# The causal mask of an attention block: from a product on TensorE to an addition in VectorE's copy of the diagonal strip

## The chip, the cores and the metric

The kernel runs on one core of a Trainium2 chip, as one program in one launch. The metric is the device time in microseconds. Five engines with queues of their own work side by side and wait for each other on semaphores: TensorE (products, PE), VectorE (DVE), ScalarE (ACT), GpSimd (POOL) and SyncE (SP), which issues the transfers.

## The reference

One transformer block with adaptive layer normalisation, on 2048 tokens of 512 features. The attention part, cut to what matters:

```python
q = einsum('bpm,hmd->bphd', x, Q_w) + Q_b        # 16 heads of 128
k = einsum('bpm,hmd->bphd', x, K_w) + K_b
v = einsum('bpm,hmd->bphd', x, V_w) + V_b
logits = einsum('bqhd,bkhd->bhqk', q, k) / sqrt(128)
logits = where(triu(ones((s, s)), k=1), -100000.0, logits)   # no query sees a later key
scores = softmax(logits, axis=-1)
attn = einsum('bhqk,bkhd->bqhd', scores, v)
out = einsum('bqhd,hdm->bqm', attn, O_w) + O_b
```

A second normalisation and a feed-forward part follow: a router that picks 4 of 64 experts per token, the experts, and two shared experts.

## The kernel before

Products of 32-bit accuracy are made of three: each operand is split into a high and a low part, and `matmul3` (L1551 to L1553) adds high by high, high by low and low by high. The probabilities and values are split in the same way into two 16-bit parts.

The attention runs head by head, and in a head in four stages, j = 0 to 3, one for each block of 512 queries. A stage has four rows, t = 0 to 3, of 128 queries. A row's logits come in j + 1 strips, one for each block of 512 keys; each strip is one PSUM bank, and four banks (`strip`) are used in turn. The last strip of a row, ch = j, lies on the diagonal: it has only (t + 1) x 128 columns, and of these the last 128 need the mask. Strips are counted over a head, 40 in all: 4, 8, 12 and 16 in the stages.

TensorE in stage (h, j) does `score(h, j)`, then `sum_values` for the stage before it (probabilities by values, into `pv`), then the projections q, k and v of the stage after it. `score` waits for `strip_out` before each strip, that is, until VectorE has copied the strip that was in that bank four strips ago, and raises `strip_done` after it. In a diagonal strip a fourth product, `ident_bf` by `mask_bf`, adds the mask's -1e5/scale above the diagonal of the last 128 columns (L1606).

VectorE in `score_row` copies each strip to `exps` (SBUF) and scales it, and takes its maximum by the way into `cmax`; the maximum is read out by a second instruction, DVE_READ_ACCUMULATOR. It then joins the maxima of the row. ScalarE takes the exponentials and their sum (L860) and makes the high part of the probabilities (`p_hi`, L869); VectorE makes the low part (`p_lo`, L1163). After the rows VectorE splits the low parts of the next q and k and of the next values (L1122, L1126, L1129).

SP issues the transposing transfers of the probabilities into `pT` (L476), 4 (j + 1) of them in a stage, strictly in order: those of rows 0 and 1, then those of rows 2 and 3. `pT` has four slots, and before the high part of rows 0 and 1 goes into a slot, SP waits on `pv_group` until the values have been summed over what the slot held. A `wait_alone` is an instruction of its own that waits and then counts a semaphore up. `sum_values` waits on `p_turned` for the slot it reads.

At the start GpSimd makes the constants `ident`, `ident_bf` and `mask_bf`. Much later, in the feed-forward part, `h2_tmp` holds a block for the second normalisation's split, `wr_sb` the router's weights, and SP loads the weights of the shared experts chunk by chunk (`load_chunk`).

Of the kernel before, what the change touches and what calls it, by code (L numbers as in the profile page):

```python
# [16 lines left out]
F32 = mybir.dt.float32  # L17
F32R = mybir.dt.float32r
BF16 = mybir.dt.bfloat16
# [3 lines left out]
ALU = mybir.AluOpType  # L23
ACT = mybir.ActivationFunctionType
AX_X = mybir.AxisListType.X
P = 128
# [15 lines left out]
def adaln_block(nc, x, Q_w, Q_b, K_w, K_b, V_w, V_b, O_w, O_b, Wr, router_bias, Wg, Wu, Wd, Sg, Su, Sd,  # L42
# [3 lines left out]
    E, _, HE = Wg.shape  # L46
# [3 lines left out]
    NT = S // P  # L50
    DC = D // P
    QB = S // 512
    TB = 4
    SC = NS * HS // P
    EPS = 1e-5
    SCALE = float(DH) ** -0.5
    MASKED = -1e5 / SCALE
# [7 lines left out]
    with ExitStack() as ctx:  # L65
        def sem(name):
            return ctx.enter_context(nc.semaphore(name))
# [4 lines left out]
        STRIPS, GENS, PTS = 4, 3, 4  # L72
        PSCALE, VMOST = 2.0 ** 14, 2.0 ** 14
        strip = [bank(f"strip{i}") for i in range(STRIPS)]
# [4 lines left out]
        base = (nc.sbuf_base + 63) // 64 * 64  # L79
        keep = SbufMap(nc, base)  # L80
        ident = keep.place("ident", [P, P], F32)
        ident_bf = keep.place("ident_bf", [P, P], BF16)
        mask_bf = keep.place("mask_bf", [P, P], BF16)
        modT = keep.place("modT", [P, 6 * DC], F32)
        scale_a = keep.place("scale_a", [P, DC], F32)
        scale_b = keep.place("scale_b", [P, DC], F32)
# [9 lines left out]
        cmax = keep.place("cmax", [P, TB, QB], F32)  # L96
# [36 lines left out]
        exps = a.place("exps", [P, TB, S], F32)  # L133
# [5 lines left out]
        spare_at = a.at  # L139
# [31 lines left out]
        o = SbufMap(nc, kqv_at)  # L171
# [5 lines left out]
        assert o.at <= v16_at, o.at  # L177
        acc = SbufMap(nc, pT_at).place("acc", [P, NT, D], F32)
        assert spare_at - pT_at >= NT * D * 4
        o = SbufMap(nc, spare_at)  # L180
        h2_tmp = o.place("h2_tmp", [P, 512], F32)
        assert o.at <= nc.sbuf_usable_end, o.at


        h2T_hi = SbufMap(nc, halves_at).place("h2T_hi", [P, DC, S], F32R)
# [6 lines left out]
        f = SbufMap(nc, w_at)  # L192
        n2 = f.place("n2", [P, 1, TB, D], F32)
        o_tmp = f.place("o_tmp", [P, D], F32)
        wr_sb = f.place("wr_sb", [P, DC, E], F32)
        s_raw = [SbufMap(nc, kqv_at - 3 * D * 4).place("s_raw0", [P, 3, D], F32)]
        assert f.at <= kqv_at - 3 * D * 4

# [2 lines left out]
        f = SbufMap(nc, kqv_at)  # L201
# [5 lines left out]
        f = SbufMap(nc, v16_at)  # L207
        s_hi[0] = f.place("s_hi0", [P, 3, D], F32R)
        s_lo[0] = f.place("s_lo0", [P, 3, D], F32R)
        assert f.at <= exps_at  # L210

        f = SbufMap(nc, hT_at)
# [62 lines left out]
        consts = sem("consts")  # L275
# [2 lines left out]
        mod_mm, mod_out = sem("mod_mm"), sem("mod_out")  # L278
        dve_step = sem("dve_step")
        pool_step = sem("pool_step")  # L280
        pool_waited, sp_waited = sem("pool_waited"), sem("sp_waited")
        tile_stat = sem("tile_stat")
        ln_stats, ln_rstd, ln_norm = sem("ln_stats"), sem("ln_rstd"), sem("ln_norm")
        ln_turned, ln_mod, ln_split = sem("ln_turned"), sem("ln_mod"), sem("ln_split")
# [5 lines left out]
        strip_done, strip_out = sem("strip_done"), sem("strip_out")  # L290
# [15 lines left out]
        wr_hi_ready, wr_split = sem("wr_hi_ready"), sem("wr_split")  # L306
# [68 lines left out]
        NSTRIP = strips_before(QB)  # L375
# [59 lines left out]
        def _(sp):  # L435
# [150 lines left out]
            h, j = H - 1, QB - 1  # L586
# [37 lines left out]
            store_n2(3)  # L624
            sp.wait_ge(ln_turned, 2 * NT)
            sp.wait_ge(n2_stored, 16 * QB)
            sp.wait_ge(wr_split, 1)
            load_chunk(3)
            load_chunk(4)

# [42 lines left out]
        def _(pool):  # L673
            steps = [0]

            def link(ins):
                steps[0] += 1
                ins.then_inc(pool_step, 1)
                pool.wait_ge(pool_step, steps[0])

            def wait_alone(semaphore, value):
# [5 lines left out]
            link(nc.gpsimd.memset(ident[:], 0.0))  # L687
            nc.gpsimd.affine_select(out=ident[:], in_=ident[:], compare_op=ALU.not_equal, fill=1.0, base=0,
                                    pattern=[[-1, P]], channel_multiplier=1).then_inc(consts, 1)
            link(nc.gpsimd.memset(ident_bf[:], 0.0))  # L690
            nc.gpsimd.affine_select(out=ident_bf[:], in_=ident_bf[:], compare_op=ALU.not_equal, fill=1.0, base=0,
                                    pattern=[[-1, P]], channel_multiplier=1).then_inc(consts, 1)
            link(nc.gpsimd.memset(mask_bf[:], 0.0))
            nc.gpsimd.affine_select(out=mask_bf[:], in_=mask_bf[:], compare_op=ALU.is_ge, fill=MASKED, base=0,
                                    pattern=[[-1, P]], channel_multiplier=1).then_inc(consts, 1)
            nc.gpsimd.memset(neghalf[:], -0.5).then_inc(consts, 1)

# [30 lines left out]
                nc.gpsimd.tensor_copy(bias_now[:], src).then_inc(bias_ready, 1)  # L728

            pool.sem_inc(v_bound, 1)  # L730
            pool.wait_ge(consts, 4)
            ln_scales(0, 0)
            pool.wait_ge(mod_out, 1)
            nc.gpsimd.tensor_copy(bias_now[:], biasT[:].rearrange("p (n h) -> p n h", n=3)[:, :, 0]
# [330 lines left out]
        def _(dve):  # L1065
# [67 lines left out]
            def value_scale(h, src):  # L1133
# [4 lines left out]
                dve.wait_ge(v_scaled_half, h + 1)  # L1138
                nc.vector.reciprocal(v_scale[:], v_most[:]).then_inc(v_scaled, 1)

            def score_row(h, j, t):
                for ch in range(j + 1):
                    u = strips_before(j) + t * (j + 1) + ch
                    w = 512 if ch < j else (t + 1) * P
                    dve.wait_ge(strip_done, h * NSTRIP + (u + 1))
                    nc.vector.tensor_scalar(exps[:, t, 512 * ch:512 * ch + w], strip[u % STRIPS][:, 0:w], SCALE, None,  # L1146
                                            ALU.mult, ALU.max, accum_out=cmax[:, t, ch:ch + 1]).then_inc(strip_out, 1)
                dve.wait_ge(strip_out, h * NSTRIP + (STRIPS + u + 1))
                nc.vector.tensor_reduce(nbias[:, t:t + 1], cmax[:, t, 0:j + 1], AX_X, ALU.max, negate=True  # L1149
                                        ).then_inc(row_logits, 1)  # L1150
# [147 lines left out]
            h, j = H - 1, QB - 1  # L1298
# [115 lines left out]
            def route_experts(s):  # L1414

                m = tiles_of(s)
                if s == 0:
                    dve.wait_ge(consts, 7)
                    link(nc.vector.tensor_copy(iota_f[:], iota_i[:]))
                for t in range(half * s, half * s + half):  # L1420
                    steps[0] += 1
                    nc.vector.max_index(idx[:, t, :], vals[:, t, :], scores[:, t, :]).then_inc(dve_step, 1)
                dve.wait_ge(dve_step, steps[0])
                link(nc.vector.tensor_copy(idx_f[:, m], idx[:, m, 0:TOPK]))
                for k in range(TOPK):
                    link(nc.vector.tensor_tensor(onehot[k][:, m], iota_f[:, 0:E].unsqueeze(1).to_broadcast([P, half, E]),
                                                 idx_f[:, m, k:k + 1].to_broadcast([P, half, E]), ALU.is_equal))
                dve.sem_inc(experts_known, 1)
# [119 lines left out]
        def _(pe):  # L1548
# [46 lines left out]
            def score(h, j):  # L1595
                pe.wait_ge(gen_out, nth("k", j, h) + GENS)
                for n, (t, ch, w) in enumerate(score_units(j)):
                    u = strips_before(j) + n
                    pe.wait_ge(strip_out, h * NSTRIP + (u + 1))
                    o = strip[u % STRIPS]  # L1600
                    rows, cols = slice(P * t, P * t + P), slice(512 * ch, 512 * ch + w)
                    last = matmul3(o[:, 0:w], qT_hi[:, rows], qT_lo[:, rows], kT_hi[:, cols], kT_lo[:, cols],
                                   True, True)
                    if ch == j:

                        last = nc.tensor.matmul(o[:, w - P:w], ident_bf[:], mask_bf[:], start=False, stop=True,  # L1606
                                                skip_group_check=True)
                    last.then_inc(strip_done, 1)

            def sum_values(h, j):  # L1610
# [37 lines left out]
                    project("v", jn, hn)  # L1648


            pe.wait_ge(consts, 4)
            pe.wait_ge(rows_landed, 48)
            nc.tensor.transpose(pv[:, 0:3 * H], bias_rows[:], ident[0:3 * H, 0:3 * H]).then_inc(mod_mm, 1)
            pe.wait_ge(c_step, 1)
# [253 lines left out]
```

## Time and profile before

| | us |
|---|---|
| median of 3 runs | 2125.84 |
| lowest and highest run | 2123.46 and 2131.11 |
| the profiled execution's own time | 2127.13 |
| its span, first to last instruction | 2125.3 |

The profile is of one execution. PE is the product engine, PEld its weight loads, which overlap products; the stated busy time of products overlaps too, since each is counted until its result is out. Busy times therefore tell which engine is full, and the distances between starts tell what an instruction costs. A row of a timeline gives start and duration in us, engine, line, operation, output and inputs, and in square brackets the idle time before it with what ended it. SPq is SP's queue, where an issue of a transfer takes time.

### The profile page before, as it was taken

How to read it: one execution, taken by the hardware profiler on the slowest of the kernel's cores; microseconds unless marked ns; L12 is line 12 of the kernel's file. 1: busy time of each engine (PE TensorE's matmuls, PEld its weight loads, DVE VectorE, ACT ScalarE, POOL GpSimd, SP SyncE). 2: the span in 40 equal slices, each digit the busy share in tenths (PEclk: the TensorE clock that was granted, in tenths of full speed). 3: DMA queues.
4: the chain of work that ended last, by engine and by line, in shares of the span. 5: the costliest groups of instructions: out<-in, count | busy, mean ns of one | idle time of the engine just before them, and what ended most of it. 6: DMA issues, size and time to landing. Idle time of an engine off the chain costs nothing.

```text
span 2125.3 us, 33337 instructions
## 1 busy us (share of the span) xinstructions
PE 2028.7 (95%) x10121; PEld 1513.4 (71%) x10121; DVE 1382.4 (65%) x3219; ACT 1106.3 (52%) x1638; POOL 387.0 (18%) x411
## 2 busy tenths in 40 slices
PE   6899999999999999999999999999999989999996
PEld 3667677676677676676776766767887768777775
DVE  7677686686686776866866866846555933333375
ACT  4566675675575665756765756533334134344310
POOL 5211010110110110100101101524001132222364
PEclk9999999999999999999999999999999999999998
DMA  6487788888878878887888889995422089999664
GB/s 213 94 163 154 158 159 162 161 157 162 168 153 168 167 153 166 160 162 159 159 162 158 161 162 176 185 205 178 135 83 65 1 253 289 318 291 319 195 206 149
DMA packets 932174, 366.08 MB, mean 172 GB/s; under 512 B 754800, under 2 KB 885920, under 8 KB 932128
## 3 DMA queue, kind: packets, MB, share of 16 engines
q1 hardware_dynamic: 921888, 331.93, 69.3%
q0 software_dynamic: 10240, 33.56, 5.1%
q8 instruction: 26, 0.43, 0.1%
q14 instruction: 20, 0.16, 0.0%
HBM read 138.86 MB, written 41.94 MB: 85 GB/s over the span
## 4 chain that ended last, share of the span: by engine, by line
PE 66%; SPq 14%; DMA 8%; DVE 5%; POOL 3%; issue 3%; ACT 1%; POOLq 0%; DVEq 0%; ACTq 0%
SPq L476 13%; PE gen L1551 9%; PE gen L1553 9%; PE gen L1552 9%; PE strip L1551 7%; PE strip L1553 7%; PE strip L1552 7%; PE pv L1551 4%; PE strip L1847 4%; PE pv L1553 4%; PE pv L1552 4%; DMA wd_sb<-in_L_ffn_Wd 3%; DMA pT<-p_lo 2%; PE strip L1854 2%; DVE acc L1533 1%
## 5 line engine op out<-in xcount | busy, mean ns | idle before, releaser
L1163 DVE SCALAR_TENSOR_TENSOR p_lo<-exps,rinv,p_hi 128x512 f16<-128x512 f32 (+3 forms) x256 | 395.6, 1560 | 23.2 <-ACT p_hi L869 21.2
L860 ACT ACTIVATE exps<-exps,nbias 128x128 f32<-128x128 f32 (+15 forms) x256 | 306.2, 1197 | 131.9 <-DVE nbias L1149 130.5
L1146 DVE TENSOR_SCALAR_CACHE_REDUCE exps<-strip 128x512 f32<-128x512 f32 (+3 forms) x640 | 359.4, 606 | 1.9 <-PE strip L1606 1.3
L869 ACT ACTIVATE p_hi<-exps,rinv 128x512 f16<-128x512 f32 (+3 forms) x256 | 338.0, 1351 | 9.5 <-DMA pT<-p_lo 3.7
L1551 PE MATMUL strip<-kT_hi,qT_hi 128*128 128x512 f32 (+3 forms) x640 | 247.7, 387 | 10.3 <-DVEq L1240 6.3
L1551 PE MATMUL pv<-pT,v 128*128 128x512 f16 (+3 forms) x640 | 222.9, 348 | 19.3 <-DMA pT<-p_lo 19.1
L1553 PE MATMUL strip<-kT_hi,qT_lo 128*128 128x512 f32 (+3 forms) x640 | 233.9, 366 | 0.0
L1552 PE MATMUL strip<-kT_lo,qT_hi 128*128 128x512 f32 (+3 forms) x640 | 233.4, 365 | 0.0
L715 POOL TENSOR_TENSOR wq_lo<-wq_raw,wq_hi 128x512 fp32r<-128x512 f32 x16 | 20.8, 1297 | 1117.8 <-ACT wq_hi L839 1117.8
L1552 PE MATMUL pv<-pT,v 128*128 128x512 f16 (+3 forms) x640 | 222.6, 348 | 0.0
L1553 PE MATMUL pv<-pT,v 128*128 128x512 f16 (+3 forms) x640 | 219.5, 348 | 0.0
L1551 PEld LDWEIGHTS strip<-kT_hi,qT_hi 128*128 128x128 f32 x640 | 122.8, 192 | 36.4 <-DVE exps L1146 7.7
L1036 ACT ACTIVATE xbT<-gen,modT,scale_b 128x128 f32<-128x128 f32 x256 | 96.3, 457 | 92.7 <-PE gen L1839 92.7
L1553 PEld LDWEIGHTS strip<-kT_hi,qT_lo 128*128 128x128 f32 x640 | 120.8, 189 | 18.8
L1122 DVE SCALAR_TENSOR_TENSOR qT_lo<-gen,bias_now,qT_hi 128x512 fp32r<-128x512 f32 x64 | 47.8, 747 | 132.6 <-ACT qT_hi L846 132.6
L1552 PEld LDWEIGHTS strip<-kT_lo,qT_hi 128*128 128x128 f32 x640 | 121.6, 190 | 17.1
L1129 DVE SCALAR_TENSOR_TENSOR vT<-gen,v_scale,vT 128x512 f16<-128x512 f32 x64 | 48.0, 750 | 125.8 <-ACT vT L854 125.6
L1551 PEld LDWEIGHTS pv<-pT,v 128*128 128x128 f16 x640 | 62.7, 98 | 89.8 <-DMA pT<-p_lo 37.1
L1491 DVE TENSOR_TENSOR hE<-strip,sil_e 128x128 f32<-128x128 f32 x64 | 18.7, 292 | 154.1 <-ACT sil_e L1043 154.1
L854 ACT ACTIVATE vT<-gen,v_scale 128x512 f16<-128x512 f32 x64 | 44.1, 688 | 136.5 <-PE gen L1553 132.8
L1551 PE MATMUL gen<-hT_hi,a_hi 128*128 128x512 f32 x256 | 101.7, 397 | 9.6 <-DVE a_lo L1282 6.1
L1551 PE MATMUL gen<-hT_hi,wq_hi 128*128 128x512 f32 x256 | 106.5, 416 | 1.8 <-issue 1.8
(240 smaller groups left out, 4410.4 us busy)
## 6 DMA issues: line engine op xcount, KB each, us to landing
at_dram<-at_f SPq DMA_DIRECT2D x64, 256.0 KB, 2.6
wg_sb<-in_L_ffn_Wg SPq DMA_DIRECT2D x64, 256.0 KB, 5.1
wu_sb<-in_L_ffn_Wu SPq DMA_DIRECT2D x64, 256.0 KB, 5.4
wd_sb<-in_L_ffn_Wd SPq DMA_DIRECT2D x64, 256.0 KB, 6.1
yb_dram<-yb SPq DMA_DIRECT2D x64, 256.0 KB, 6.0
a_f<-at_dram SPq DMA_DIRECT2D x58, 256.0 KB, 2.8
pT<-p_hi SPq DMA_TRANSPOSE x320, 3.3
pT<-p_lo SPq DMA_TRANSPOSE x320, 3.3
```

The costliest lines, as they stand in the source:

```text
L476: sp.dma_start_transpose(out, rows).then_inc(p_turned[slot_of(j, g)], 16)
L860: nc.scalar.activation(row, row, ACT.Exp, bias=nbias[:, t:t + 1], accum_out=rsum[:, t:t + 1]).then_inc(row_probs, 1)
L869: nc.scalar.activation(p_hi16[:, 0:j + 1, t, :], row, ACT.Copy, scale=rinv[:, t:t + 1]).then_inc(p_hi, 1)
L1036: ins = nc.scalar.activation(xbT[:, i % 2, P * ch:P * ch + P], e_turn[:, P * ch:P * ch + P], ACT.Identity, bias=modT[:, 3 * DC + ch:3 * DC ...
L1122: ins = nc.vector.scalar_tensor_tensor(qT_lo[:], src[:], bias_now[:, 0:1], qT_hi[:].bitcast(F32), ALU.add, ALU.subtract)
L1129: ins = nc.vector.scalar_tensor_tensor(vT16[:, 1, :], src[:], v_scale[:, 0:1], vT16[:, 0, :], ALU.mult, ALU.subtract)
L1146: nc.vector.tensor_scalar(exps[:, t, 512 * ch:512 * ch + w], strip[u % STRIPS][:, 0:w], SCALE, None, ALU.mult, ALU.max, accum_out=cmax[:, ...
L1163: nc.vector.scalar_tensor_tensor(p_lo16[:, 0:j + 1, t, :], row, rinv[:, t:t + 1], p_hi16[:, 0:j + 1, t, :], ALU.mult, ALU.subtract).then_i ...
L1551: nc.tensor.matmul(o, a_hi, b_hi, start=start, stop=False)
L1552: nc.tensor.matmul(o, a_hi, b_lo, start=False, stop=False)
L1553: return nc.tensor.matmul(o, a_lo, b_hi, start=False, stop=stop)
L1847: last = nc.tensor.matmul(e_gateup[i % 2][:, P * n:P * n + P], w[:, i % EX, c, :], xbT[:, i % 2, P * c:P * c + P], start=c == 0, stop=c == ...
```

## The change

The mask leaves TensorE. `causal` is a constant of 4 x 128 columns in bfloat16: zeros, and in its last 128 columns the mask. For a diagonal strip of w columns VectorE now uses an operation with two inputs: the strip plus the last w columns of `causal`, times the scale, with the running maximum as before. The wait for the strip is an instruction of its own ahead of it. The other strips are copied as before. `ident_bf` and `mask_bf` are gone; `causal` takes 512 bytes more per partition than both, and so `h2_tmp` and `wr_sb` move into other buffers. Since `h2_tmp` now lies where chunk 3 of the shared weights lands, SP waits for the last split of the second normalisation before it loads that chunk.

```diff
-        ident_bf = keep.place("ident_bf", [P, P], BF16)
-        mask_bf = keep.place("mask_bf", [P, P], BF16)
+        causal = keep.place("causal", [P, TB * P], BF16)
...
-        o = SbufMap(nc, spare_at)
-        h2_tmp = o.place("h2_tmp", [P, 512], F32)
...
-        wr_sb = f.place("wr_sb", [P, DC, E], F32)
+        h2_tmp = f.place("h2_tmp", [P, 512], F32)
...
+        wr_sb = f.place("wr_sb", [P, DC, E], F32)
...
-            sp.wait_ge(wr_split, 1)
+            sp.wait_ge(ln_split, 2 * NT)
             load_chunk(3)
...
-            link(nc.gpsimd.memset(ident_bf[:], 0.0))
-            nc.gpsimd.affine_select(out=ident_bf[:], in_=ident_bf[:], compare_op=ALU.not_equal, fill=1.0, base=0,
-                                    pattern=[[-1, P]], channel_multiplier=1).then_inc(consts, 1)
-            link(nc.gpsimd.memset(mask_bf[:], 0.0))
-            nc.gpsimd.affine_select(out=mask_bf[:], in_=mask_bf[:], compare_op=ALU.is_ge, fill=MASKED, base=0,
+            diagonal = causal[:, (TB - 1) * P:TB * P]
+            link(nc.gpsimd.memset(causal[:], 0.0))
+            nc.gpsimd.affine_select(out=diagonal, in_=diagonal, compare_op=ALU.is_ge, fill=MASKED, base=0,
                                     pattern=[[-1, P]], channel_multiplier=1).then_inc(consts, 1)
...
+            def wait_alone(semaphore, value):
+
+                dve.wait_ge(semaphore, value)
+                dve.sem_inc(dve_waited, 1)
+
             def score_row(h, j, t):
                 for ch in range(j + 1):
                     u = strips_before(j) + t * (j + 1) + ch
                     w = 512 if ch < j else (t + 1) * P
-                    dve.wait_ge(strip_done, h * NSTRIP + (u + 1))
-                    nc.vector.tensor_scalar(exps[:, t, 512 * ch:512 * ch + w], strip[u % STRIPS][:, 0:w], SCALE, None,
-                                            ALU.mult, ALU.max, accum_out=cmax[:, t, ch:ch + 1]).then_inc(strip_out, 1)
+                    if ch < j:
+                        ...
+                    else:
+
+                        wait_alone(strip_done, h * NSTRIP + (u + 1))
+                        nc.vector.tensor_tensor_reduce(exps[:, t, 512 * ch:512 * ch + w], strip[u % STRIPS][:, 0:w],
+                                                       causal[:, TB * P - w:TB * P], SCALE, -3e38, ALU.add, ALU.max,
+                                                       cmax[:, t, ch:ch + 1]).then_inc(strip_out, 1)
...
-                    if ch == j:
-
-                        last = nc.tensor.matmul(o[:, w - P:w], ident_bf[:], mask_bf[:], start=False, stop=True,
-                                                skip_group_check=True)
                     last.then_inc(strip_done, 1)
```

## Rows read from the trace of the kernel before

**Rows 1.** The page: busy time of TensorE, and the chain that ended last, by engine.
```profile
PE 2028.7 (95%) x10121; PEld 1513.4 (71%) x10121; DVE 1382.4 (65%) x3219; ACT 1106.3 (52%) x1638; POOL 387.0 (18%) x411
...
PE 66%; SPq 14%; DMA 8%; DVE 5%; POOL 3%; issue 3%; ACT 1%; POOLq 0%; DVEq 0%; ACTq 0%
```

**Rows 2.** Stretches: stretch, length, busy time by engine, PEclk; a middle and the last head.
```profile
479.24:562.17 82.93, 81.65 (x405) 59.04 (x404) 60.76 (x158) 53.00 (x69) 7.00 (x6) 1.00 0.82 161
1316.90:1399.80 82.90, 75.10 (x363) 55.16 (x361) 62.55 (x135) 47.55 (x57) 43.20 (x32) 1.00 0.96 202
```

**Rows 3.** The chain in order of time, stage 3 and after: start, us, what.
```profile
553.81 0.07 PE pv L1553
...
553.97 1.23 SPq L476
...
570.45 3.16 DMA pT<-p_lo
...
573.66 0.39 PE pv L1551
```

**Rows 4.** Timeline of TensorE in stage 3 around a mask between two rows.
```profile
541.23 0.23 PE L1606 MATMUL strip<-mask_bf,ident_bf 128*128 128x128 bf16 x1
541.26 0.48 PE L1551 MATMUL strip<-kT_hi,qT_hi 128*128 128x512 f32 x1
...
542.05 0.39 PE L1551 MATMUL strip<-kT_hi,qT_hi 128*128 128x512 f32 x1
...
542.74 0.39 PE L1551 MATMUL strip<-kT_hi,qT_hi 128*128 128x512 f32 x1
```

**Rows 5.** The same timeline at the end of stage 3's strips.
```profile
546.83 0.23 PE L1606 MATMUL strip<-mask_bf,ident_bf 128*128 128x128 bf16 x1
546.89 0.38 PE L1551 MATMUL pv<-pT,v 128*128 128x512 f16 x1
```

**Rows 6.** Timelines of TensorE and VectorE at the fifth strip of stages 1 and 2.
```profile
502.85 0.23 PE L1606 MATMUL strip<-mask_bf,ident_bf 128*128 128x128 bf16 x1
503.12 0.50 PE L1551 MATMUL strip<-kT_hi,qT_hi 128*128 128x512 f32 x1
...
502.98 0.08 DVE L1146 DVE_READ_ACCUMULATOR exps<-strip 128x1 f32 x1
...
518.38 0.44 PE L1551 MATMUL strip<-kT_hi,qT_hi 128*128 128x512 f32 x1
...
518.19 0.08 DVE L1146 DVE_READ_ACCUMULATOR exps<-strip 128x1 f32 x1
```

**Rows 7.** Timelines of SP and VectorE in stage 3.
```profile
548.62 6.58 SPq L476 DMA_TRANSPOSE pT<-p_hi  x4
...
554.18 4.61 DVE L1163 SCALAR_TENSOR_TENSOR p_lo<-exps,rinv,p_hi 128x2048 f16<-128x2048 f32 x2 [0.65 <-ACT p_hi L869]
```

**Rows 8.** The chain in order of time: a lone wait in SP's queue.
```profile
560.82 0.02 SPq L439
560.84 0.05 issue
```

**Rows 9.** Groups by line and shape: busy us, mean ns of one, idle before.
```profile
L1146 DVE TENSOR_SCALAR_CACHE_REDUCE exps<-strip 128x512 f32<-128x512 f32 x448 | 289.6, 685 | 0.6 <-PE strip L1553 0.6
...
L1497 DVE TENSOR_TENSOR yb<-strip,gb_bc 128x512 f32<-128x512 f32 x64 | 44.2, 690 | 14.5 <-PE strip L1854 14.3
...
L1352 DVE TENSOR_TENSOR hs_lo<-sil_s,hs_hi 128x512 fp32r<-128x512 f32 x32 | 22.6, 706 | 12.6 <-ACT hs_hi L995 12.6
...
L1146 DVE TENSOR_SCALAR_CACHE_REDUCE exps<-strip 128x128 f32<-128x128 f32 x64 | 18.2, 285 | 0.6 <-PE strip L1606 0.6
```

**Rows 10.** Timelines of VectorE and TensorE, first strip of row 3 in stage 3.
```profile
543.55 0.08 DVE L1146 DVE_READ_ACCUMULATOR exps<-strip 128x1 f32 x1
...
544.00 0.47 PE L1551 MATMUL strip<-kT_hi,qT_hi 128*128 128x512 f32 x1
```

**Rows 11.** Timelines of SP and VectorE at the shared weights' chunk 3.
```profile
1604.33 0.37 SPq L582 DMA_DIRECT2D s_raw<-in_L_ffn_Sg  x1
...
1608.16 0.69 DVE L1252 TENSOR_TENSOR h2T_lo<-h_tmp,h2T_hi 128x512 fp32r<-128x512 f32 x1 [1.58 <-ACT h_tmp L976]
```

More of the change, by code:

```diff
@@ L179, in adaln_block @@
         assert spare_at - pT_at >= NT * D * 4
-        o = SbufMap(nc, spare_at)
-        h2_tmp = o.place("h2_tmp", [P, 512], F32)
-        assert o.at <= nc.sbuf_usable_end, o.at
         h2T_hi = SbufMap(nc, halves_at).place("h2T_hi", [P, DC, S], F32R)
@@ L280, in adaln_block @@
         pool_step = sem("pool_step")
-        pool_waited, sp_waited = sem("pool_waited"), sem("sp_waited")
+        pool_waited, sp_waited, dve_waited = sem("pool_waited"), sem("sp_waited"), sem("dve_waited")
         tile_stat = sem("tile_stat")
@@ L730, in _ @@
             pool.sem_inc(v_bound, 1)
-            pool.wait_ge(consts, 4)
+            pool.wait_ge(consts, 3)
             ln_scales(0, 0)
@@ L1144, in score_row @@
                     w = 512 if ch < j else (t + 1) * P
-                    dve.wait_ge(strip_done, h * NSTRIP + (u + 1))
-                    nc.vector.tensor_scalar(exps[:, t, 512 * ch:512 * ch + w], strip[u % STRIPS][:, 0:w], SCALE, None,
-                                            ALU.mult, ALU.max, accum_out=cmax[:, t, ch:ch + 1]).then_inc(strip_out, 1)
+                    if ch < j:
+                        dve.wait_ge(strip_done, h * NSTRIP + (u + 1))
+                        nc.vector.tensor_scalar(exps[:, t, 512 * ch:512 * ch + w], strip[u % STRIPS][:, 0:w], SCALE,
+                                                None, ALU.mult, ALU.max, accum_out=cmax[:, t, ch:ch + 1]
+                                                ).then_inc(strip_out, 1)
+                    else:
[3 more added lines that the diff above has]
+                                                       cmax[:, t, ch:ch + 1]).then_inc(strip_out, 1)
                 dve.wait_ge(strip_out, h * NSTRIP + (STRIPS + u + 1))
@@ L1417, in route_experts @@
                 if s == 0:
-                    dve.wait_ge(consts, 7)
+                    dve.wait_ge(consts, 6)
                     link(nc.vector.tensor_copy(iota_f[:], iota_i[:]))
@@ L1648, in stage @@
                     project("v", jn, hn)
-            pe.wait_ge(consts, 4)
+            pe.wait_ge(consts, 3)
             pe.wait_ge(rows_landed, 48)
```

## The prediction

> **What bounds the kernel now.** I read the page first: TensorE is busy 95% of the span, and the chain of work that ended last runs 66% through TensorE and 14% through SP's own queue [rows 1]. TensorE is therefore the first suspect, but the second share says that somewhere it waits for transfers. The stretches say where the change acts: the masks exist only in the attention of 16 heads, and a head from the middle, 479.24 to 562.17, takes 82.93 us with TensorE at its full granted clock (1.00), busy 81.65 us, VectorE only 60.76 [rows 2]. Then I followed the chain through that head. It leaves TensorE at one place: when the value products of stage 2's probabilities end (553.81 + 0.07), SP may reuse the slot of transposed probabilities and issues stage 3's fourth transpose at 553.97; 12 more follow back to back, the last at 570.45, landing 3.16 us later, and only then, at 573.66, does TensorE go on [rows 3]. In between TensorE did other work (the next head's projections and its four score strips of stage 0) and then stood, so that work is not on the chain. A head is a ring: TensorE from 573.66 through stages 1, 2 and 3 up to the end of the stage-2 values, then SP. A saving counts if it falls in the TensorE part of the ring.
>
> **What the change removes on TensorE.** 16 mask products per head, 4 in each stage. Their busy time is no price, since products overlap. The starts give it. A mask starts at 541.23, the next row's first product at 541.26, which is 0.03; that next strip then takes 542.05 - 541.26 = 0.79, where a strip after no mask takes 542.74 - 542.05 = 0.69 [rows 4]. The 0.10 is the weight load of the next row, which the short mask product is too short to cover. So a mask between two rows costs 0.03 + 0.10 = 0.13 us. The last mask of a stage is followed by a value product 0.06 later [rows 5] and I find no second term there: 0.06.
>
> The Trainium skill bears on the first figure: "TensorE: Matmul & The Clock Gate", section "Back-to-back issue gap", gives about 81 ns per product of 128 columns in a stream of load and product pairs, where the trace shows 0.13. By that page the eight masks counted below would be worth 8 x 0.08 x 15 = 9.7 us; I keep the trace.
>
> **Which masks are on the ring.** Stage 0's four lie in the stretch that ends in the wait for the transposes: nothing. In stages 1 to 3 VectorE starts to copy strips only after it has split the projected values that come in just before them, and there are four strip banks, so the fifth strip waits for the first to be copied. In stage 1 a mask starts at 502.85 and the next strip only at 503.12, 0.06 after the accumulator read that frees its bank ends (502.98 + 0.08) [rows 6]. Masks ahead of that point only make TensorE arrive earlier at the same gate: rows 0 and 1 in stage 1, row 0 in stage 3 likewise. In stage 2 the fifth strip starts at 518.38, 0.11 after its bank came free (518.19 + 0.08) [rows 6]: 0.05 could be won there, but TensorE would then have the next weights loaded only when the gate opens, as in stage 1, so I put nothing. What is left: stage 1, one mask between rows and the last, 0.13 + 0.06 = 0.19; stage 2, two between and the last, 0.32; stage 3 likewise 0.32. Together 0.83 us per head. Both ends of this term: 8 x 0.03 = 0.24 if only the masks' own slots count, and 12 x 0.13 + 4 x 0.06 = 1.8 if all 16 do.
>
> Does the saving in stage 3 pass on to SP? SP's first four transposes there take 6.58 us from 548.62 [rows 7]; four of 1.23 (the fourth's length [rows 3]) are 4.92, and the rest, 1.66 with three gaps, is mostly waiting for value groups. There is more than 0.32 to take back. The rows that follow are not late either: the last two parts of the probabilities are ready at 554.18 + 4.61 = 558.79, while the transposes that need them come after 560.8 [rows 7, 8].
>
> **What it adds on VectorE.** 16 copies per head change from a one-input operation with a running maximum (685 ns for 512 columns, 285 for 128) to a two-input one with scaling and a maximum. The trace of before has no such operation. The nearest rows are two-input ones from the same kind of bank: 690 ns for 512 columns [rows 9]. I take 5 ns more. Bounds: below, the 0.08 of the accumulator read could go; above, half rate: the slope is (685 - 285) / 384 = 1.04 ns per column, so up to 0.53 more at 512 columns and 0.13, 0.27, 0.40 at the narrower ones. The lone wait ahead of each copy is one more instruction. SP's, of the same make, take 0.02 with 0.05 behind them [rows 8]; VectorE's queue is ahead of its datapath while it copies back to back, so I take 0, bounds 0 and 0.07. What hides VectorE's extra: it is 60.76 busy in 82.93, and before each stage's strips it stands for the value part; and no gate strip above is a diagonal one. Where cover ends is the tightest bank behind the gate: in stage 3 the strip at 544.00 uses a bank freed at 543.55 + 0.08, a slack of 0.37 [rows 10]. With the masks gone TensorE comes 0.16 sooner (one whole mask, 0.13, and one slot, 0.03), and 0.06 is the least gap, so VectorE may be 0.15 late there. Two diagonal copies lie before it, so each may cost 0.07 more for nothing: with my 0.005 the loss is zero, and so it is with the whole 0.07 of the lone wait.
>
> **The rest of the diff.** GpSimd makes two constants instead of three before VectorE's first statistics: both hide behind the load of the input, 0. SP's chunk 3 of the shared weights now waits for the last split of the second normalisation: the load went at 1604.33, the split ends at 1608.16 + 0.69, so 4.5 us later [rows 11]. Queued behind it on SP are chunk 4, which waits for a later split anyway, and the expert loads, which wait for routing; the chunk is first read in step 10 of the twelve that begin there. 0, and if it delayed chunk 4 it would be a microsecond. The moved buffers carry the same transfers.
>
> **Sum.** The ring exists for heads 0 to 14: 15 x 0.83 = 12.5 us. Head 15 has its weights for the output projection loading between the transposes and GpSimd busy 43.20 us instead of 7.00; TensorE is busy only 75.10 of 82.90 there [rows 2], so I put 0. The profiled execution took 2127.13 (span 2125.3), which gives 2114.6; the median of the three times is 2125.84, 1.3 below the profiled one, which gives 2113.3. I say 2113.
>
> **Rivals.**
> All masks count: if the wait at 573.66 shrinks too and the gates move, 16 heads at 1.8 give 29 us, 2097. Against: the gates' 0.06 and the twelve back-to-back transposes, which no mask touches.
> Stage 3 gives nothing, because SP or ScalarE is late by then and the ring's SP part starts no sooner: 0.51 x 15 = 7.7, 2118. For it: everything SP does in stage 3 is queued in order. Against: the time SP spends waiting in its first four [rows 7].
> The new operation runs at half rate. Then 0.13 + 0.27 = 0.40 come before the tight strip against 0.15 allowed, a loss of 0.25 in stage 3, taken to be the same in stage 2, none in stage 1: 0.83 - 0.50 = 0.33 a head, 5.0 us, 2121. Against: a subtraction with both inputs in SBUF takes 706 ns for 512 columns [rows 9], no half rate. The Trainium skill warns of this: "Vector Engine (DVE) Microarchitecture Reference", section "Points that are easy to get wrong", says that one kind of instruction with two non-bf16 SBUF sources halves its throughput. Here one source is a PSUM bank and the other is bf16, so by its own words it need not bind, and the trace does not show it.
> Slower: a fixed cost x per diagonal copy, from a slow start of this new kind of operation or from a wait that VectorE's queue cannot run ahead of. It holds back the strips at the tight banks: 2x - 0.15 in stages 2 and 3, and x - 0.15 in stage 1 (one diagonal copy before the strip behind the gate, slack taken alike), together 5x - 0.45 against 0.83: it decides from x = 0.26 us. At x = 0.5 the head loses 1.2 us, 18 in all, 2144. Against: all of VectorE's known operations on such a bank have the same fixed part: 0.285 less 128 x 1.04 ns is 0.15, and 0.690 less 512 x 1.04 ns is 0.16 [rows 9].
> That the masks are really gone from TensorE is plain from the diff.
>
> **Chances.** Forecast 0.54, all masks 0.07, stage 3 gives nothing 0.14, half rate 0.13, slower 0.09, and 0.03 for what I don't see. A measurement of this kernel tells 0.5%, 10.6 us, from no change, so faster means below 2115.2. Of the forecast's own range, 2109 to 2117, about four fifths lie there. Faster 0.43 + 0.07 = 0.50; same: a fifth of the forecast, 0.11, with stage 3 and half rate, 0.27, and part of the unseen, 0.40; slower 0.10. The range 2102 to 2126 leaves out the slower case and the far end of the full saving.
>
> **What would show it.** The strip behind a row's end should take 0.69 instead of 0.79 and start where the mask did; the fifth strip of stages 1 to 3 should still start 0.06 after its bank is freed; a head should take 82.1 us; TensorE's stand before the last value group of stage 3 should grow, since stage 0's masks now go into it. The diagonal copy should read about 690 ns at 512 columns. If a head is at 82.93 with VectorE's strips late, the operation is dear; if it is near 81, the gates are not what I take them for.

## The result, and the profile after

Over four executions each, shared on one chip, the changed kernel takes 2113.12 us (median; 2111.54 to 2119.06), the kernel before 2125.95 (2123.46 to 2131.11). The ratio is 0.9942, 95% interval 0.9914 to 0.9969: faster by 0.6%. The forecast was 2113, from 2102 to 2126. The profiled execution of after happens to be its slowest, 2119.06, so the time is compared by heads below and not by the two spans.

The page, busy time of TensorE and VectorE and the chain by engine (answers to [rows 1]):
```profile
PE 2014.0 (95%) x9863; PEld 1501.2 (71%) x9865; DVE 1381.3 (65%) x3219; ACT 1103.8 (52%) x1638; POOL 386.7 (18%) x409
...
PE 65%; SPq 15%; DMA 8%; DVE 4%; issue 4%; POOL 3%; ACT 1%; DVEq 0%; POOLq 0%; ACTq 0%
```
258 TensorE records fewer (256 of them would be the masks), and the chain has the same shape: TensorE gave up 14.7 us of busy time, VectorE's is the same to 1.1 us.

The two stretches of [rows 2]: the middle head, from its first score strip to the next head's, and the last head, where the stretch is taken as long and as far behind the head's first strip (8.4 us) as in before.
```profile
473.11:555.39 82.28, 80.66 (x389) 58.17 (x388) 60.70 (x158) 52.89 (x69) 7.00 (x6) 1.00 0.83 163
1304.13:1387.03 82.90, 75.30 (x350) 55.56 (x348) 62.36 (x135) 47.43 (x57) 42.05 (x32) 0.98 0.94 200
```
The middle head went from 82.93 to 82.28 (82.1 was forecast). The last head's first strip starts at 1295.77 instead of 1308.54, so 12.8 us are won by then. Behind it the profiled execution gives 4.7 back: 821.5 us to its end against 816.8. That part takes 816 to 822 in the profiles of this study, whatever the kernel, so one execution does not say whose it is.

The ring of [rows 3], in the chain of waits of the same head:
```profile
547.04 0.07 PE pv L1561
...
547.20 1.23 SPq L473
...
563.72 3.31 DMA pT<-p_lo
...
567.08 0.39 PE pv L1559
```
It is unbroken: stage 2's values end, SP issues 13 transposes, TensorE goes on 0.04 behind the last landing. From the fourth transpose to there it is 19.88 us, before 19.69: SP's part did not get shorter.

TensorE's timeline in stage 3 around the place where the mask between two rows was (answers to [rows 4]), and at the end of its strips [rows 5]:
```profile
534.64 0.28 PE L1561 MATMUL strip<-kT_hi,qT_lo 128*128 128x256 f32 x1
534.76 0.40 PE L1559 MATMUL strip<-kT_hi,qT_hi 128*128 128x512 f32 x1
...
535.46 0.40 PE L1559 MATMUL strip<-kT_hi,qT_hi 128*128 128x512 f32 x1
...
536.14 0.39 PE L1559 MATMUL strip<-kT_hi,qT_hi 128*128 128x512 f32 x1
...
539.88 0.39 PE L1561 MATMUL strip<-kT_hi,qT_lo 128*128 128x512 f32 x1
540.12 0.39 PE L1559 MATMUL pv<-pT,v 128*128 128x512 f16 x1
```
The strip that opens a row takes 535.46 - 534.76 = 0.70 where it took 0.79: the exposed weight load is gone with the mask. The weight loads themselves say it too, before and after:
```profile
541.23 0.20 PEld L1551 LDWEIGHTS strip<-kT_hi,qT_hi 128*128 128x128 f32 x1
```
```profile
534.64 0.19 PEld L1559 LDWEIGHTS strip<-kT_hi,qT_hi 128*128 128x128 f32 x1
```
The load for the row's first product starts 0.03 before that product in before (541.26) and 0.12 before it in after (534.76).

The gates at the fifth strip of stages 1 and 2, TensorE and VectorE (answers to [rows 6]):
```profile
497.15 0.50 PE L1559 MATMUL strip<-kT_hi,qT_hi 128*128 128x512 f32 x1 [0.19 <-DVE exps L1147]
...
512.18 0.51 PE L1559 MATMUL strip<-kT_hi,qT_hi 128*128 128x512 f32 x1
```
```profile
497.01 0.08 DVE L1147 DVE_READ_ACCUMULATOR exps<-strip 128x1 f32 x1
...
512.04 0.08 DVE L1147 DVE_READ_ACCUMULATOR exps<-strip 128x1 f32 x1
```
Stage 1's strip starts 0.06 after the read that frees its bank, as before; stage 2's now does too (0.06, before 0.11). The masks ahead of a gate bought nothing.

VectorE's copies by form (busy us, mean ns of one; answers to [rows 9]), and the first strip of row 3 in stage 3 with the read that frees its bank [rows 10]:
```profile
L1147 DVE TENSOR_SCALAR_CACHE_REDUCE exps<-strip 128x512 f32<-128x512 f32 x384 | 249.1, 685 | 1.8 <-PE strip L1561 1.8
...
L1153 DVE CUSTOM_DVE_ANT_0 exps<-strip,causal 128x512 f32<-128x512 f32 x64 | 44.0, 687 | 1.5 <-PE strip L1561 0.3
...
L1153 DVE CUSTOM_DVE_ANT_0 exps<-strip,causal 128x384 f32<-128x384 f32 x64 | 35.4, 553 | 1.4
...
L1153 DVE CUSTOM_DVE_ANT_0 exps<-strip,causal 128x256 f32<-128x256 f32 x64 | 26.9, 421 | 1.7 <-PE strip L1561 0.2
...
L1153 DVE DVE_READ_ACCUMULATOR2_ANT cmax<- 128x1 f32 x256 | 21.2, 83 | 0.0
...
L1153 DVE CUSTOM_DVE_ANT_0 exps<-strip,causal 128x128 f32<-128x128 f32 x64 | 18.2, 284 | 0.6 <-PE strip L1561 0.6
```
```profile
537.08 0.08 DVE L1147 DVE_READ_ACCUMULATOR exps<-strip 128x1 f32 x1
...
537.35 0.40 PE L1559 MATMUL strip<-kT_hi,qT_hi 128*128 128x512 f32 x1
```
The new operation takes 687 ns for 512 columns beside 685 for the plain copy, and 284 for 128 where it was 285. The slack at the tight bank is 537.35 - 537.16 = 0.19, where it was 0.37: half used up, not gone.

To see where the time came from, each stage is measured from its first score strip to the next stage's, mean over heads 2 to 14, worked out from the starts in the trace of each run. The last column is the chip's ratio to the kernel before.

```
kernel                        stage 0   1      2      3     head   time     ratio [95%]
before                        21.47  15.22  20.36  25.88   82.93  2125.95
after                         21.59  15.02  20.04  25.58   82.24  2113.12  0.9942 [0.9914, 0.9969]
e1_again                      21.55  15.02  20.05  25.56   82.19  2115.12  0.9934 [0.9921, 0.9948]
e2_no_mask                    21.55  15.02  20.05  25.57   82.19  2113.73  0.9925 [0.9912, 0.9939]
e3_hidden8                    21.56  15.02  20.06  25.57   82.21  2115.58  0.9936 [0.9922, 0.9949]
e4_ring8                      21.55  15.21  20.35  25.89   83.00  2128.79  0.9998 [0.9988, 1.0008]
e5_both                       21.58  15.20  20.36  25.89   83.04  2127.87  1.0004 [0.9994, 1.0015]
e6_delay64                    21.57  15.01  20.32  26.22   83.12  2129.32  1.0008 [0.9996, 1.0021]
e7_delay320                   21.56  15.85  20.33  26.75   84.49  2153.18  1.0128 [1.0106, 1.0150]
e8_late_after                 20.14  15.02  20.05  25.58   80.79  2094.46  0.9852 [0.9836, 0.9869]
e9_q_first                    19.61  16.73  20.05  25.58   81.96  2116.41  0.9947 [0.9934, 0.9960]
e10_q_first_old_mask          20.05  17.64  20.35  25.90   83.93  2146.02  1.0082 [1.0067, 1.0097]
e11_q_first_stage0            20.05  17.10  20.05  25.58   82.77  2124.77  0.9983 [0.9971, 0.9995]
e12_values_later              19.61  15.52  20.04  26.74   81.90  2108.70  0.9903 [0.9889, 0.9917]
```
In e10 and e11 the means mix two kinds of heads, as shown with them. e1 to e4 shared a chip and runs of before with median 2129.4, e5 to e8 2128.12, e9 to e12 2128.61; times of different groups are compared by ratio.

### The profile page after: what moved, and what is told of

It reads as the page before. It is cut to its first block, busy times and chain, and to the rows that moved or that the text cites. A ratio compares the mean times of both kernels' runs of the same rounds, so it can differ in the third digit from the quotient of the medians.

```text
span 2117.3 us, 33076 instructions
## 1 busy us (share of the span) xinstructions
PE 2014.0 (95%) x9863; PEld 1501.2 (71%) x9865; DVE 1381.3 (65%) x3219; ACT 1103.8 (52%) x1638; POOL 386.7 (18%) x409
## 4 chain that ended last, share of the span: by engine, by line
PE 65%; SPq 15%; DMA 8%; DVE 4%; issue 4%; POOL 3%; ACT 1%; DVEq 0%; POOLq 0%; ACTq 0%
SPq L473 14%; PE gen L1559 9%; PE gen L1561 9%; PE gen L1560 9%; PE strip L1559 7%; PE strip L1560 6%; PE strip L1561 6%; PE strip L1851 4%; PE pv L1559 4%; PE pv L1561 3%; PE pv L1560 3%; DMA wd_sb<-in_L_ffn_Wd 3%; DMA pT<-p_lo 2%; PE strip L1858 2%; DVE acc L1541 1%
## 5 line engine op out<-in xcount | busy, mean ns | idle before, releaser
L1559 PE MATMUL strip<-kT_hi,qT_hi 128*128 128x512 f32 (+3 forms) x640 | 238.3, 372 | 14.4 <-DVEq L1248 6.3
L1147 DVE TENSOR_SCALAR_CACHE_REDUCE exps<-strip 128x512 f32<-128x512 f32 x384 | 249.1, 685 | 1.8 <-PE strip L1561 1.8
L1153 DVE CUSTOM_DVE_ANT_0 exps<-strip,causal 128x128 f32<-128x128 f32 (+3 forms) x256 | 124.5, 486 | 5.2 <-PE strip L1561 1.1
```

Of the source, the lines that this page charges most:

```text
L1153: nc.vector.tensor_tensor_reduce(exps[:, t, 512 * ch:512 * ch + w], strip[u % STRIPS][:, 0:w], causal[:, TB * P - w:TB * P], SCALE, -3e38, ...
L1559: nc.tensor.matmul(o, a_hi, b_hi, start=start, stop=False)
```

## The experiments

**The changed kernel once more** (e1), for a firmer interval beside the others. 

> The changed kernel once more, for a firm ratio. Ring theory (only masks behind the fifth strip of stages 1, 2 and 3 count): a head takes 82.2 us, 0.7 less than before, and the time is 12 us below the kernel before, about 2114. Rival (the first measurement was luck of the feed-forward part, where two executions differ by some us): the ratio comes out at 0.998 or above.


Measured: 2115.12, ratio 0.9934. The first result stands, a head is 82.19.

**No mask on either engine** (e2): the kernel before, with the product left out. Its output lacks the causal mask.
```diff
-                    if ch == j:
-                        last = nc.tensor.matmul(o[:, w - P:w], ident_bf[:], mask_bf[:], start=False, stop=True,
-                                                skip_group_check=True)
```


> The kernel before without the mask product, and no mask anywhere: VectorE copies as before. This is the gain of TensorE's part alone. If VectorE's new operation costs nothing: the same as the changed kernel, 2114, a head 82.2. If the new operation and its lone wait give part of the gain back: below the changed kernel, by 0.07 x 5 x 15 = 5 us or more.


Measured: 82.19 a head, ratio 0.9925 [0.9912, 0.9939], e1's 0.9934 [0.9921, 0.9948]. The intervals overlap: VectorE's mask with its lone waits, the fewer constants and the moved buffers cost nothing that can be measured. The traces of before and after say the same: VectorE's copies of stage 3 take 9.674 and 9.671 us from the start of the first to that of the last.

**Eight masks back on TensorE ahead of the gates** (e3), **or eight behind them** (e4), on top of VectorE's own. The product adds the zero part of the constant, so it has the old size and changes no value.
```diff
                                    True, True)
+                    if ch == j and t <= (3, 1, 0, 0)[j]:    # e4: t > (3, 1, 0, 0)[j]; e5: always
+                        last = nc.tensor.matmul(o[:, w - P:w], causal[:, 0:P], causal[:, 3 * P:4 * P], start=False,
+                                                stop=True, skip_group_check=True)
                     last.then_inc(strip_done, 1)
```


> The changed kernel with a product of the mask's size that adds zeros put back in 8 of 16 rows: all of stage 0, rows 0 and 1 of stage 1, row 0 of stages 2 and 3. Ring theory: these are ahead of a gate or of the wait for the transposes, so nothing, a head 82.2, 2114. Rival (every mask product costs the same share of TensorE's time): half of the gain goes, a head 82.6, 2120.

> The changed kernel with the same product put back in the other 8 rows: rows 2 and 3 of stage 1, rows 1 to 3 of stages 2 and 3. Ring theory: the whole gain goes, a head 82.9, 2126. Rival (equal shares): half, a head 82.6, 2120.


A head of each, from its first strip to the next head's:
```profile
473.85:556.19 82.34, 80.84 (x397) 58.68 (x396) 60.70 (x158) 52.89 (x69) 7.00 (x6) 1.00 0.83 162
```
```profile
476.73:559.76 83.03, 81.45 (x397) 58.51 (x396) 60.77 (x158) 53.00 (x69) 7.00 (x6) 1.00 0.82 161
```
Both run 397 products; they differ only in where the eight stand. The first eight cost 0.02 a head by the table (82.21 beside 82.19), the other eight 0.81 (83.00), and 0.19, 0.30 and 0.33 of it lie in stages 1, 2 and 3. On the chip e3 keeps the whole gain and e4 has none of it. This is what set the ring apart from a plain sum over products, by which both would have lost the same. The Trainium skill's "TensorE: Matmul & The Clock Gate", section "Back-to-back issue gap", would make the eight 8 x 0.081 = 0.65; the heads of e3 and e4 differ by 0.79 in the table, so here the page's figure comes out too small. By [rows 4] and [rows 5] one figure does not fit both places: the five between rows are priced at 0.13, the three at a stage's end at 0.06, together 0.83.

**All sixteen back** (e5), the new VectorE operation kept. 

> The changed kernel with a product that adds zeros put back in all 16 rows, so that only VectorE's side differs from the kernel before. If VectorE's side costs nothing: as before, 2126, a head 82.9. If the new operation costs x more than the 0.1 or so that the tightest banks have to give: above, by 5x a head.


Measured: 83.04 a head, ratio 1.0004. The whole gain is the products'; nothing else in the diff has a part of it that the interval, 0.9994 to 1.0015, would show.

**A dearer diagonal copy** (e6 and e7): a small VectorE addition between the lone wait and the copy, 64 or 320 columns, into a buffer that nothing reads.
```diff
                         wait_alone(strip_done, h * NSTRIP + (u + 1))
+                        nc.vector.tensor_tensor(junk[:, 0:64], ga_bc[:, 0:64], gb_bc[:, 0:64], ALU.add)   # e7: 0:320
                         nc.vector.tensor_tensor_reduce(...
```


> The changed kernel with an addition of 64 columns on VectorE, into a scratch buffer, ahead of each of the 16 diagonal copies of a head: x = 64 x 1.04 ns + 0.07 = 0.14 us each. Ring theory with the slacks read in the changed kernel (first strip of row 3: 0.19 in stage 3, second strip of row 3: 0.16 in stage 2, least gap 0.06, two diagonal copies ahead of each): 2x - 0.13 + 2x - 0.10 = 0.33 a head, 5 us, 2118. If VectorE, busy three quarters of a head, has room: 0. If its work were all on the path: 16x = 2.2 a head, 33 us.

> The same with 320 columns: x = 0.40 us. Ring theory: 2x - 0.13 and 2x - 0.10 in stages 3 and 2, x - 0.27 in stage 1, 1.5 a head, 23 us, 2137, slower than the kernel before; the break-even lies near x = 0.23. With room on VectorE: 0. All on the path: 6.4 a head, 96 us.


Measured: ratios 1.0008 and 1.0128; against the changed kernel a head loses 0.9 and 2.3 us. The slower rival's mechanism is real. The strips that it names now start the instant their bank is free: the slack at row 3's first strip in stage 3, 0.19 in the changed kernel, is 0.055 in both. The loss sits in stages 2 and 3 for e6 (0.28 and 0.64, expected 0.18 and 0.15). For e7 it is 0.83, 0.29 and 1.17 in stages 1, 2 and 3, where 0.13, 0.70 and 0.67 were expected: both sums came out too small, and e7's was also placed wrongly. The groups of the added operation, busy us and mean ns of one:
```profile
L1154 DVE TENSOR_TENSOR junk<-ga_bc,gb_bc 128x64 f32<-128x64 f32 x256 | 66.8, 261 | 2.9 <-PE strip L1563 0.6
```
```profile
L1154 DVE TENSOR_TENSOR junk<-ga_bc,gb_bc 128x320 f32<-128x320 f32 x256 | 131.2, 512 | 2.8 <-PE strip L1563 0.6
```
From its start to the next operation's it takes 0.138 and 0.404 us as a median (worked out from the starts), the sizes meant. But e6 loses more than such a size gives, and for stage 3 the reason is in two of the sixteen additions, rows 0 and 2. VectorE and GpSimd at row 2:
```profile
544.27 0.60 DVE L1154 TENSOR_TENSOR junk<-ga_bc,gb_bc 128x64 f32<-128x64 f32 x1
544.79 0.55 DVE L1155 CUSTOM_DVE_ANT_0 exps<-strip,causal 128x384 f32<-128x384 f32 x1
```
```profile
543.48 1.30 POOL L711 TENSOR_TENSOR wv_lo<-wv_raw,wv_hi 128x512 fp32r<-128x512 f32 x1
```
The addition took 0.60 instead of 0.22, and the copy behind it starts at 544.79, as GpSimd's subtraction ends (543.48 + 1.30 = 544.78). The addition reads two tensors of SBUF while GpSimd reads two. The Trainium skill states this ("SBUF — State Buffer", section "Terms": the pair of ports that the two engines share is held for the full instruction, and the loser "fully blocks"), and by these rows the trace agrees. It does not at row 1, where the GpSimd operation reads one tensor of SBUF only:
```profile
540.35 1.92 POOL L718 TENSOR_SCALAR wv_abs<-wv_raw 128x512 bf16<-128x512 f32 x1
...
541.42 0.22 DVE L1154 TENSOR_TENSOR junk<-ga_bc,gb_bc 128x64 f32<-128x64 f32 x1
```
The addition lies wholly inside that operation and takes its usual 0.22, in each of the 15 heads where the two meet. So the measurement decides for a narrower rule: held up beside a two-input operation of GpSimd, not beside this one-input one. The new copy reads one bank and one SBUF tensor and was never held up: the longest of 256 took 693 ns, and 34 of them overlap a two-input subtraction of GpSimd. So in stage 3 row 0's addition cost 0.38 and row 2's 0.52 in place of 0.14, by VectorE's row lengths (2.654 against 2.277, 3.360 against 2.844). Why stage 2 lost 0.10 more than expected stays open.

e7's loss in stage 1 comes mostly by a wait that the expectation had not counted. TensorE at the first strip of stage 2:
```profile
522.30 0.39 PE L1563 MATMUL gen<-hT_hi,wv_lo 128*128 128x512 f32 x1
523.05 0.49 PE L1561 MATMUL strip<-kT_hi,qT_hi 128*128 128x512 f32 x1 [0.36 <-DVE kT_lo L1122]
```
VectorE, late by then, has not split the low part of k, and TensorE takes 0.75 from start to start where such products follow each other in 0.23: 0.52 of the 0.83, and the like in each of heads 2 to 14 (0.33 to 0.38 idle there, none in after).

**Where stage 0's masks went** (e8). In the trace of after TensorE stands before the last value group of stage 3, and that is where the time freed in stage 0 ends:
```profile
565.45 0.38 PE L1561 MATMUL pv<-pT,v 128*128 128x512 f16 x1
567.08 0.39 PE L1559 MATMUL pv<-pT,v 128*128 128x512 f16 x1 [1.26 <-DMA pT<-p_lo]
```
Over heads 2 to 14 these stands are 1.8 us a head, 1.45 in before. e8 moves other work into them: the last group goes behind the next head's query projection.
```diff
-                    sum_values(hp, jp)
+                    late = jp == QB - 1 and nxt is not None
+                    sum_values(hp, jp, range(0, QB - 1) if late else None)
                 if nxt is not None:
                     hn, jn = nxt
                     project("q", jn, hn)
+                    if prev is not None and late:
+                        sum_values(hp, jp, range(QB - 1, QB))
                     project("k", jn, hn)
```


> The changed kernel, but in the stage after stage 3 TensorE makes the next q projection (2.7 us) before the last value group instead of after it, so that it works while the last transposes land. Ring theory: the stand of about 1.7 us a head goes and the ring closes through TensorE alone: a head 80.5, 25 us less, 2088. Rival (the last transposes are not what the head waits for, or a later wait takes over, such as the q parts arriving late for the scores): 2110 or more.


Measured: 2094.46, ratio 0.9852 [0.9836, 0.9869], the fastest kernel of the study. A head is 80.79, and all of the difference to e1 is in stage 0 (21.55 to 20.14). That is 1.4 of the 1.7 expected; 0.31 a head is left in short stands ahead of the first three groups.

**The query projection ahead of all value groups** (e9), to take the rest.
```diff
                 score(h, j)
+                early = prev is not None and prev[1] == QB - 1 and nxt is not None
+                if early:
+                    project("q", nxt[1], nxt[0])
                 if prev is not None:
...
-                    project("q", jn, hn)
+                    if not early:
+                        project("q", jn, hn)
```


> The changed kernel, with the next q projection made before all four value groups of stage 3, not between the third and the fourth. What was left of the stand there, 0.3 us in short waits ahead of the first three groups, should go: a head 80.4 instead of 80.8, 5 us less, 2089. Rival (those short gaps are not waits for transposes): 80.8, 2094.


Measured: 81.96 a head, ratio 0.9947. That expectation fell: no stand is left in the values of stage 3, stage 0 shrinks to 19.61 as it should, and stage 1 gives back 1.7. The chain of waits of e9 between two stages says by what way (parts that lie between are left out):
```profile
732.40 0.23 PE pv L1561
...
732.71 1.24 SPq L473
...
738.47 3.10 DMA v<-vT
741.59 0.70 ACT vT L849
742.31 0.05 DVE vT L1124
...
743.58 0.09 DVE exps L1147
...
743.72 0.50 PE strip L1559
```
The end of value group 3 of 4 (732.40) frees the slot of stage 0's first transpose; four transposes and, behind them in SP's queue, the turning of the values follow; ScalarE's next value buffer waits for that landing (741.59), then VectorE's split, its first copy, and the gate at stage 1's fifth strip. In e8, counted from stage 0's first strip of the same head, SP passes the first wait at 10.61 us and ScalarE starts at 20.33; in e9 at 12.63 and 21.58. Work moved ahead of group 3 shifts a second ring that had slack.

**The same with the old mask** (e10, the kernel before with e9's edit) **and with stage 0's four masks alone** (e11, e9 with the zero products for `j == 0`), to see whether the masks of stage 0 are worth something once their stand is filled.


> The same reordering in the kernel before the change, mask product and all. Ring theory: with the wait for the transposes gone, stage 0's four masks are on the path too, 3 x 0.13 + 0.06 = 0.45 a head, so the gap between the two mask forms grows from 0.75 to 1.2 a head, 18 us: a head 81.6, 2107. Rival (stage 0's masks cost nothing of themselves): the gap stays 0.75, 11 us, 81.15, 2100.

> e9's kernel with a product of the mask's size that adds zeros put back in the four rows of stage 0 only. Ring theory: 0.45 a head, 80.85, 7 us above e9, where the same four (with four more) cost nothing while the wait was there. Rival: nothing.


Measured: e11 is 0.81 a head slower than e9 (ratio 0.9983 against 0.9947), e10 1.97. So the four masks that were worth nothing cost 0.44 in stage 0 here, as expected, and 0.37 more in stage 1, not expected. The 0.44 is visible all along the second ring (SP's wait passes at 13.07 instead of 12.63, ScalarE's start is 22.07 instead of 21.58). The 0.37 is not a cost of every head. Stage 1 of two neighbouring heads of e11, with its length, busy times and granted clock:
```profile
415.68:434.01 18.33, 16.43 (x74) 12.65 (x73) 12.99 (x35) 11.00 (x16) 0.00 (x0) 0.91 0.79 168
499.70:516.45 16.75, 14.84 (x74) 11.80 (x73) 12.77 (x35) 10.87 (x16) 0.00 (x0) 1.00 0.77 166
```
In the first of them the granted clock is at the lower of TensorE's two levels, 1.2 instead of 2.4 GHz, for some 3 us:
```profile
421.20:424.40 3.20, 3.20 (x9) 1.93 (x8) 2.93 (x13) 3.02 (x5) 0.00 (x0) 0.50 0.81 215
```
This happens in 3 of e11's heads 2 to 14, which take 84.04, and in 6 of e10's, which take 84.80. The other heads take 82.39 and 83.19, and those are 0.43 and 1.23 above e9, where none of heads 2 to 14 has such a fall: as differences both expectations, 0.45 and 1.2, hold in the heads at the full clock (the head times stated with them counted from an e9 of 80.4), and the rest of the difference is the clock's, about 1.6 us a head where it falls. TensorE had stood 1.9 us at the fifth strip and gone on when it fell (419.80, then 421.1), but it stands as long there in every head of e11 and e9; what decides in which head the clock falls is not shown. The mean granted clock of whole executions is 0.982 to 0.985 in e11 and 0.980 to 0.984 in e10, and 0.983 to 0.988 in e9, whose profiled execution is the one with 0.988, so the chip's ratios hold some of it as well.

**The values' split behind the first score row** (e12, on top of e9), to take the second ring off the gate.
```diff
             def stage(h, j, nxt, first=False):
                 score_row(h, j, 0)
+                if not first:
+                    gen_out_of("v", j, h)
                 score_row(h, j, 1)
...
                         value_scale(hn, pv[:, 0:1])
-                    gen_out_of("v", jn, hn)
```


> e9's kernel, with VectorE's split of the values moved behind its first row of strips, so that it starts to copy some 0.9 us sooner and the gate at the fifth strip opens sooner. TensorE's stand there (0.35 in stage 1, 0.08 in stage 2, 0.04 in stage 3) and the late weight load of the strip at the gate (0.1 each) go: 0.77 a head, 12 us, 2077. Rival (the gates cost less than they seem, or the values then arrive late for their transposes and the stand moves there): 2085 or more.


Measured: 81.90 a head, 2108.70, ratio 0.9903: better than e9, not near the expectation. Stage 1 falls from 16.73 to 15.52, but stage 3 rises from 25.58 to 26.74. Its chain of waits there:
```profile
530.36 0.76 DVE vT L1124
...
531.76 0.62 ACT wk_hi L834
532.38 0.52 ACT wv_hi L834
532.90 0.65 ACT exps L855
...
534.79 0.05 DVE rinv L1166
...
534.91 0.11 DVE exps L1147
...
535.66 0.50 PE strip L1561
```
In stage 3 ScalarE may split the next head's weights only when VectorE's split of the values is done. These halves now come ahead of row 0's exponentials instead of before the strips; VectorE waits for those in row order before it copies row 2, and the strip behind waits for VectorE.

## Why the prediction was right, and where its sizes were off

- **The ring.** Right, and shown by e3 and e4: eight products cost nothing and eight of the same kind 0.81 a head, stage by stage where they were counted.
- **The price of a mask**, 0.13 between rows and 0.06 at a stage's end. Right: stages 1, 2 and 3 lost 0.20, 0.32 and 0.30, forecast 0.19, 0.32, 0.32. The view that gave it, starts of products and not their busy time, was the right one: 16 masks of 0.23 would be 3.7 us a head.
- **Does stage 3's saving pass to SP?** It does: e4 loses 0.33 in stage 3, and stage 0, which holds the wait for SP's transposes, is as long with it as without (21.55 in e4 and e1). Had SP started no sooner, stage 0 would have grown by what stage 3 saved.
- **The ring's sum, 0.83 a head.** Right between kernels of one build: with all products back (e5) a head is 83.04, without (e1) 82.19, a difference of 0.85. Against the one trace of before it is less, 0.69 (0.74 for e1), since stage 0 is shorter in that trace: 21.47, where it is 21.55 to 21.59 in all eight with an unchanged order (after, e1 to e7), with its four masks (e3, e5) and without (e1, e2, e4). So it is not the masks. e2 is the kernel before less the products and has 21.55 as well, which points to an execution's difference; before was not profiled again, and this stays open.
- **Heads 2 to 14** therefore gave 13 x 0.69 = 9.0 of the forecast's 10.8 in the profiled pair. Its total still came out because heads 0 and 1 gave 3.8, where 1.7 was counted. 1.5 to 2.4 of that is head 1 of before, 85.59 us, where e5, with the same products, has 84.12 and e4 83.17. The row of its stage 0 shows what is special, a granted clock of 0.93:
```profile
144.82:168.95 24.13, 21.95 (x101) 14.11 (x100) 8.47 (x27) 8.21 (x18) 0.00 (x0) 0.93 0.91 164
```
The stage takes 22.64 in e5 and 21.72 in e4, where the clock is full. So in the profiled pair the fit of the total is luck of about 2 us.
- **The new operation**, 5 ns more, bounds 0 to 0.53. Measured 0 to 2 ns. The half-rate rival and the 0.07 for the lone wait are out by e2.
- **The slower rival's break-even at 0.26 us a copy.** Not far off: e6, 0.14 at most places and 0.24 to 0.38 more at two of the sixteen, lands on the time of before (1.0008). But e7 at 0.40 lost 2.3 a head where the rival's 5x less 0.45 gives 1.6, so the formula misses a wait, TensorE's for the low part of k. A smooth 0.26 was not tried.
- **The tight bank**: 0.37 less 0.16 should leave 0.21; 0.19 is there.
- **Gates stay at 0.06**: yes, and stage 2's strip joined them, as was foreseen.
- **Chunk 3 and the last head, put at zero.** Not told apart. What comes behind the start of head 15 differs by 5 us between executions of like kernels.

## What to carry to other kernels

Before a saving on the busiest engine is counted, find the ring it stands in: what lies ahead of a gate or of a stand costs nothing and gives nothing. Price a short product by the starts around it, with the weight load that it leaves uncovered. A stand that takes in a saving is the next thing to fill, but work moved into it must not pass a point for which another queue waits: with the projection ahead of the last value group alone the gain is 1.5% (e8), with it ahead of all four, and so of the third, on which SP waits, it is 0.5% (e9). And before a mean over heads is explained, look whether the heads agree and at their granted clock.

## What the runs showed of the hardware that was not expected

- The two-input copy with scale and maximum runs at the one-input copy's pace: (687 - 284) / 384 = 1.05 ns a column with a float32 bank and a bf16 SBUF tensor, and its accumulator read is 83 ns like the other's.
- An fp32 addition of 64 columns from SBUF takes 0.22 us, and up to 0.61 when GpSimd is in a two-input operation, but 0.22 when GpSimd is in a one-input one (e6). GpSimd's own was stretched as well: in e7 its subtraction for k, behind row 0's addition of 320 columns, takes 1.54 instead of 1.30 us in 15 of 16 heads.
- The lone wait in VectorE's queue with its semaphore increment cost nothing (e1 against e2), though it stands ahead of 256 copies.
- The granted clock fell to half for some 3 us in stage 1 of 3 of 13 heads in e11 and of 6 of 13 in e10, at about 1.6 us each. TensorE had stood 1.7 to 2.0 us just before. In e8, where it stands 0.19 at that strip, there was no such fall.
